# Expert jobs of 128 rows instead of 256 in a transformer kernel with two mixture-of-experts layers

## Chip, cores and metric

The kernel runs on one core of one Trainium2 chip. The metric is the device time of one execution in microseconds (us); the median of three runs is given. Everything is float32 unless a tile is said to be bfloat16.

## What is computed

The input x has 16 sequences of 256 rows with 128 features. Three layers of causal attention with 16 heads follow each other; the second and the third have an expert network behind them. The one that matters here is the second layer's: each row chooses its own two experts out of 8.

```
def _token_moe(h, gw, gb, w1, b1, w2, b2):
    cw = _combine_weights(h @ gw + gb)          # softmax over the two best of 8
    out = jnp.zeros_like(h)
    for e in range(E):
        out = out + _ffn(h, w1[e], b1[e], w2[e], b2[e]) * cw[..., e:e + 1]
    return out

def _ffn(h, w1, b1, w2, b2):                    # 128 -> 512 -> 128
    return jax.nn.gelu(h @ w1 + b1, approximate=False) @ w2 + b2

x = x + _layernorm(_attn_ref(_layernorm(x)))
x = x + _layernorm(_ffn_ref(_layernorm(x)))     # two layers: attention + experts
```

In the third layer a whole sequence chooses its two experts (`_seq_moe`). The change doesn't touch that one.

## The kernel before

The program has four parts on every engine. First come the first two attention layers (`run_steps` over `RUNS[0]`), one sequence after the other. In the second of them each row's normalised vector is sent to a buffer in HBM, `x_routed`, at a place that depends on its expert and on its rank among the rows of this expert; GpSimd (POOL) does that with indirect DMAs (`pool_send`). Then come the expert jobs of that layer, then the third attention layer, which begins by fetching each row's two results from `y_routed` (`pool_fetch`), then the experts of the third layer.

A job is a block of T = 256 consecutive rows of `x_routed` that belong to one expert. 4096 rows with two experts each are 8192 row visits; since every expert's last block may be partly empty, the program always runs JOBS = 2 x 16 + 8 = 40 jobs, the last of them on zeros if they aren't needed. `dve_tables` (L1014) works out on VectorE (DVE), in a chain in which each instruction waits for the one before, how many blocks each expert has, and from this the expert and first row of every job (`job_e`, `job_row`, L1043 to L1060). It also gives the place after each expert's last row (`pad_row`), where `pads` (L1293) writes a block of zeros, four experts from SyncE's queue (SP) and four from ScalarE's (ACT).

The jobs run as a software pipeline over five engines, each with its own loop made by `run_jobs` (L1199): two bodies written out, a loop of two bodies, and the last jobs written out.

- SP (`sp_jobs`, L1300): in the body of job j it reads job j+4's row from the table (`value_load`), waits until the transposes of job j+2 are done, and loads 256 rows into `xj[par]`, one of two buffers. Then it waits for job j's sum (`acc`) and stores `yj[par]` into `y_routed`.
- PE, the TensorE (`pe_jobs`, L1216): transposes the rows of job j+2 (`rows_T`, L1221, two instructions), makes the hidden layer of job j+1 (`pe_hidden`, L1150: four matmuls of 256 columns, each two instructions), and the output of job j (`pe_output`, L1161: eight matmuls of 128 columns, each two instructions). In the profile these stages are "W1" = L1150 and "W2" = L1161.
- ACT (`act_jobs`, L1241): copies job j+2's transposed rows out of PSUM with scale and bias (L1245), and does the four Gelu instructions of job j+1 (L1172).
- POOL (`pool_jobs`, L1262): reads job j+2's expert from the table, waits until job j's hidden layer is done, and copies the expert's w1 (512 elements in each partition) into `w1_job[par]` (L1180).
- DVE (`dve_jobs`, L1273): reads job j+2's expert (L1196), waits for job j's Gelu and copies b1 (L1193, 4 elements), waits for job j's output and adds b2 to it into `yj[par]` (L1280), waits for that add, and copies w2 (L1187, 512 elements) and b2 (L1188) of job j+2.

`need(engine, semaphore, value)` is a wait that is left out where the value is zero or less, `alone(engine)` a semaphore increment that is there to carry a wait. `times` gives the count at which a buffer's load or store is over. Each tile of two buffers has the index `par`, the parity of the job.

Of the kernel before, what the change touches and what calls it, by code (L numbers as in the profile page):

```python
# [15 lines left out]
P = 128  # L16
# [4 lines left out]
E = 8  # L21
# [22 lines left out]
def build(nc, x_in, w_qk, w_v, w_o, b_qk, b_v, b_o, ln1, ln2, gate_w, gate_b, e_w1, e_b1, e_w2, e_b2, out):  # L44
# [7 lines left out]
    MAXJ = B  # L52
    JOBS = TOP * B + E
    REG = (MAXJ + 1) * T
# [3 lines left out]
    with ExitStack() as ctx:  # L58
# [102 lines left out]
        tb = prob1[:, 0].rearrange("p h q -> p (h q)")  # L161
        assert max(JOBS * E, NT * TOP * E) <= HG * P
# [6 lines left out]
        zeros = sb("zeros", [P, 2, P])  # L169

        xj = oT[:, 0, 0:2].rearrange("p i (t d) -> p i t d", t=2)
# [5 lines left out]
        x_routed = nc.dram_tensor("x_routed", [E * REG + T, P], F32, kind="Internal").ap()  # L177
        y_routed = nc.dram_tensor("y_routed", [JOBS * T, P], F32, kind="Internal").ap()
# [24 lines left out]
        x_got = [sem("x_got0"), sem("x_got1")]  # L203
# [714 lines left out]
        def pool_fetch(i, n):  # L918

            u = i.v - 2 * B  # L920
            t, rank = divmod(n, TOP)
            if n == 0:
                pool.wait_ge(table, NTABLE)
                if isinstance(i.v, int) and i.b < 2:
                    for par in range(2):
                        pool.wait_ge(y_sent[par], 8 * JOBS)
# [87 lines left out]
        def dve_tables():  # L1014
# [19 lines left out]
            step(nc.vector.scalar_tensor_tensor(out=t, in0=t, scalar=1.0 / T,  # L1034
# [19 lines left out]
            step(nc.vector.scalar_tensor_tensor(out=row, in0=row, scalar=float(T), in1=spare, op0=ALU.mult,  # L1054
# [16 lines left out]
            step(nc.vector.scalar_tensor_tensor(out=flat[2], in0=flat[0], scalar=float(T), in1=flat[1],  # L1071
# [83 lines left out]
        def pe_output(j, par):  # L1155
# [10 lines left out]
        def act_gelu(j, par):  # L1166
            need(act, y_ps, j - 1)
            act.wait_ge(b1_got, j + 1)
            for c in range(FC):
                if c % 2 == 0:  # L1170
                    act.wait_ge(h_ps, 2 * j + c // 2 + 1)
                nc.scalar.activation(hid[:, par, c], bank[2 * par + c // 2][:, (c % 2) * T:(c % 2 + 1) * T],  # L1172
                                     ACT.Gelu, bias=b1_job[:, par, c:c + 1]).then_inc(gelu_done, 1)
# [38 lines left out]
        def times(j, par):  # L1212

            return 8 * (j + (2 if par == 0 else 1))

        def pe_jobs():  # L1216
            def rows_T(j, par):
                pe.wait_ge(x_got[par], times(j, par))
                need(pe, xjT_sb, j - 1)
                for t in range(2):  # L1220
                    m = nc.tensor.transpose(bank[6 + par][:, t * P:(t + 1) * P], xj[:, par, t], ident[:])  # L1221
                m.then_inc(xjT_ps, 1)

            def hidden(j, par):
                pe.wait_ge(xjT_sb, j + 1)
                pe_hidden(j, par, xjT[:, par])

            def body(j, par):
                if ahead(j, 2):
                    rows_T(j + 2, par)  # L1230
                if ahead(j, 1):
                    hidden(j + 1, 1 - par)
                pe_output(j, par)
# [7 lines left out]
        def act_jobs():  # L1241
            def rows_T(j, par):
                act.wait_ge(xjT_ps, j + 1)
                need(act, h_ps, 2 * j - 2)
                nc.scalar.activation(xjT[:, par], bank[6 + par][:, 0:T], ACT.Identity,  # L1245
                                     scale=ln2_s[:, 0, 0:1], bias=ln2_s[:, 0, 1:2]).then_inc(xjT_sb, 1)

            def body(j, par):
                if ahead(j, 2):
                    rows_T(j + 2, par)  # L1250
                if ahead(j, 1):
                    act_gelu(j + 1, 1 - par)
# [3 lines left out]
            act_gelu(0, 0)  # L1256
# [5 lines left out]
        def pool_jobs():  # L1262
            def body(j, par):
                if ahead(j, 2):
                    pool_w1(j + 2, par, entry(job_e, j + 2))
# [7 lines left out]
        def dve_jobs():  # L1273
            def body(j, par):
                if ahead(j, 2):
# [17 lines left out]
        def pads(eng, experts):  # L1293

            for e in experts:
                row = eng.value_load(pad_row[0:1, e:e + 1], min_val=0, max_val=E * REG - T)
                eng.dma_start(x_routed[bass.ds(row, T)].rearrange("(t p) d -> p t d", p=P), zeros[:])\
                   .then_inc(pad_dma, 16)

        def sp_jobs():  # L1300

            def load(j, par):
                row = nc.sync.value_load(entry(job_row, j), min_val=0, max_val=E * REG)
                need(sp, xjT_ps, j - 1)
                alone(sp)
                sp.dma_start(xj[:, par], x_routed[bass.ds(row, T)].rearrange("(t p) d -> p t d", p=P))\
                  .then_inc(x_got[par], 16)

            def body(j, par):
# [13 lines left out]
            for j in range(4):  # L1323
                load(j, j % 2)
            run_jobs(sp, body, 4)
# [139 lines left out]
        def _(_):  # L1465
            sp.dma_start(x_all[:, 0:8], x_dram[:, 0:8]).then_inc(x_first, 16)
            for t, d in ((ln1_s, ln1), (wqk_s, w_qk), (wv_s, w_v)):
# [3 lines left out]
            sp.dma_start(x_routed[E * REG:E * REG + T].rearrange("(t p) d -> p t d", p=P), zeros[:])\  # L1471
              .then_inc(zeros_dma, 16)
# [182 lines left out]
```

## Time and profile before

| | us |
|---|---|
| median of three runs | 1273.79 |
| lowest and highest of them | 1273.51, 1277.96 |
| the profiled execution's own time | 1271.35 |
| its span, from the first to the last instruction | 1269.6 |
| mean granted clock of TensorE in it | 0.943 of full speed |

The profile is of one execution. The busy time of an engine counts its data instructions; value loads, register operations, branches and semaphore waits are not in it, but they have rows of their own under the name of the queue (DVEq, SPq).
### The profile page before, as it was taken

How to read it: one execution, taken by the hardware profiler on the slowest of the kernel's cores; microseconds unless marked ns; L12 is line 12 of the kernel's file. 1: busy time of each engine (PE TensorE's matmuls, PEld its weight loads, DVE VectorE, ACT ScalarE, POOL GpSimd, SP SyncE). 2: the span in 40 equal slices, each digit the busy share in tenths (PEclk: the TensorE clock that was granted, in tenths of full speed). 3: DMA queues.
4: the chain of work that ended last, by engine and by line, in shares of the span. 5: the costliest groups of instructions: out<-in, count | busy, mean ns of one | idle time of the engine just before them, and what ended most of it. 6: DMA issues, size and time to landing. Idle time of an engine off the chain costs nothing. (4 is left out here: it accounts for less than half of the span.)

```text
span 1269.6 us, 36493 instructions
## 1 busy us (share of the span) xinstructions
PE 1064.3 (84%) x10172; PEld 795.5 (63%) x10267; DVE 936.9 (74%) x2774; ACT 767.8 (60%) x1745; POOL 663.6 (52%) x986
## 2 busy tenths in 40 slices
PE   1888999999999899998199997387888989959997
PEld 0565666666666666665199997255655656638996
DVE  3678999999988889997523332278889888865665
ACT  1566777777777777776066564156657667645554
POOL 3345565566556777776611111566676666422332
PEclk8899999999999999999599999589989899988999
DMA  5332111111112122211222222243221211100000
GB/s 148 93 96 78 51 49 38 42 49 52 53 52 59 45 64 63 67 51 37 75 63 70 70 70 71 56 115 103 76 65 39 65 47 55 53 2 9 17 21 21
DMA packets 120793, 74.57 MB, mean 59 GB/s; under 512 B 7936, under 2 KB 115712, under 8 KB 120704
## 3 DMA queue, kind: packets, MB, share of 16 engines
q1 hardware_dynamic: 101536, 54.48, 15.5%
q10 hardware_dynamic: 15072, 10.61, 2.9%
q0 software_dynamic: 4096, 8.40, 2.2%
q8 instruction: 43, 0.70, 0.2%
q14 instruction: 46, 0.38, 0.1%
HBM read 22.21 MB, written 12.71 MB: 28 GB/s over the span
## 5 line engine op out<-in xcount | busy, mean ns | idle before, releaser
L608 DVE TENSOR_REDUCE negm<-bank 128x2 f32<-128x512 f32 (+1 forms) x576 | 389.1, 679 | 84.2 <-PE bank L300 59.0
L496 ACT ACTIVATE prob<-bank 128x512 f32<-128x512 f32 x576 | 339.7, 595 | 126.6 <-PE bank L322 88.5
L889 POOL TENSOR_SCALAR_AFFINE_SELECT prob<-prob 128x512 f32<-128x512 f32 x384 | 248.3, 648 | 171.3 <-ACT prob L496 169.1
L341 PE MATMUL bank<-prob,vaug 128*32 128x256 f32 (+1 forms) x3072 | 168.7, 338 | 1.6 <-POOL prob L889 1.3
L308 PE MATMUL bank<-stack 126*128 126x256 bf16 x768 | 152.3, 280 | 0.0
L327 PE MATMUL bank<-stack 128*128 128x256 bf16 x768 | 150.7, 278 | 0.9 <-ACT prob L496 0.9
L1180 POOL COPY w_job<-w_s 128x512 f32 x72 | 47.1, 655 | 191.7 <-PE bank L1150 183.0
L1161 PEld LDWEIGHTS bank<-w_job,prob 128*128 128x128 f32 x1152 | 139.6, 192 | 3.6
L1161 PE MATMUL bank<-w_job,prob 128*128 128x128 f32 x1152 | 139.9, 275 | 0.0
L341 PEld LDWEIGHTS bank<-prob,vaug 128*32 128x32 f32 x3072 | 81.6, 111 | 78.5 <-issue 46.7
L1172 ACT ACTIVATE prob<-bank,b_job 128x256 f32<-128x256 f32 x288 | 118.2, 469 | 16.4 <-PE bank L1150 15.1
L304 PE MATMUL bank<-maskneg,identb 128*128 128x256 bf16 x384 | 109.2, 284 | 2.7 <-DVE negm L608 2.7
L507 ACT COPY mT<-bank 8x256 bf16<-8x256 bf16 x192 | 68.4, 356 | 55.7 <-PE bank L352 52.5
L322 PE MATMUL bank<-stack 128*128 128x128 bf16 x768 | 75.5, 220 | 21.3 <-DMA stack<-mT 19.1
L300 PE MATMUL bank<-stack 126*128 126x128 bf16 x768 | 75.9, 221 | 20.3 <-DMA stack<-parts 8.9
L327 PEld LDWEIGHTS bank<-stack 128*128 128x128 bf16 x768 | 75.3, 99 | 13.4 <-ACT prob L496 1.5
L352 PE MATMUL bank<-identb,mparts 128*8 128x128 bf16 x384 | 53.4, 221 | 35.8 <-DVE mparts L617 34.9
L914 POOL DMA_INDIRECT x_routed<-hk,x_at x64 | 64.9, 1014 | 34.5 <-DVE x_at L769 16.6
L308 PEld LDWEIGHTS bank<-stack 126*128 126x128 bf16 x768 | 77.3, 101 | 8.3 <-issue 0.6
L1150 PE MATMUL bank<-oT,w_job 128*128 128x256 f32 x320 | 77.4, 386 | 0.0
L300 PEld LDWEIGHTS bank<-stack 126*128 126x128 bf16 x768 | 60.5, 99 | 25.0 <-issue 1.7
L933 POOL DMA_INDIRECT y_got<-y_routed,y_at x64 | 63.7, 995 | 22.4 <-POOL y_at L930 12.3
(180 smaller groups left out, 2003.7 us busy)
## 6 DMA issues: line engine op xcount, KB each, us to landing
stack<-parts SPq DMA_DIRECT2D x288, 128.0 KB
w_s<-e_w ACTq DMA_DIRECT2D x32, 256.0 KB, 2.9
oT<-x_routed SPq DMA_DIRECT2D x40, 128.0 KB, 2.1
y_routed<-oT SPq DMA_DIRECT2D x40, 128.0 KB, 1.8
stack<-mT SPq DMA_DIRECT2D x192, 4.0 KB
out<-x_all SPq DMA_DIRECT2D x16, 128.0 KB, 1.8
b_all<-e_b ACTq DMA_DIRECT2D x2, 512.0 KB, 8.3
x_routed<-hk,x_at POOLq DMA_INDIRECT x64, 2.3
```

The source lines that it names most:

```text
L300: m = nc.tensor.matmul(o[:, h], q[:, p0 + h, 0:P], k[:, p0 + h, 0:P], start=False, stop=True, skip_group_check=True)
L304: nc.tensor.matmul(o[:, :, P:T], identb[:], maskneg[:, 0:2], start=True, stop=False, skip_group_check=True)
L308: m = nc.tensor.matmul(o[:, h], q[:, hh, P:T], k[:, hh, :], start=False, stop=True, skip_group_check=True)
L322: m = nc.tensor.matmul(bk[:, h * P:(h + 1) * P], k[:, p0 + h, P:T], q[:, p0 + h, P:T], start=True, stop=True)
L327: m = nc.tensor.matmul(bk[:, h * T:(h + 1) * T], k[:, hh, 0:P], q[:, hh, :], start=True, stop=True)
L341: m = nc.tensor.matmul(o, w, (prob0, prob1)[kb][:, g % 2, h], start=kb == 0, stop=kb == 1, skip_group_check=True)
L496: nc.scalar.activation(o, s, ACT.Exp, scale=SCALE).then_inc(exp_done, 1)
L608: nc.vector.tensor_reduce(o, s, AX.X, ALU.max, negate=True).then_inc(max_done, 1)
L889: nc.gpsimd.affine_select(out=t, in_=t, compare_op=ALU.is_ge, fill=0.0, base=0, pattern=[[0, HG], [1, P]], channel_multiplier=-1).then_inc ...
L1150: m = nc.tensor.matmul(bank[2 * par + c // 2][:, (c % 2) * T:(c % 2 + 1) * T], w1_job[:, par, c * P:(c + 1) * P], rows, start=True, stop=True)
L1161: m = nc.tensor.matmul(bank[4 + par][:, t * P:(t + 1) * P], hid[:, par, c, t * P:(t + 1) * P], w2_job[:, par, c], start=(c == 0), stop=(c ...
L1172: nc.scalar.activation(hid[:, par, c], bank[2 * par + c // 2][:, (c % 2) * T:(c % 2 + 1) * T], ACT.Gelu, bias=b1_job[:, par, c:c + 1]).the ...
```

## The change

The jobs have P = 128 rows. There are JOBS = 2 x 32 + 8 = 72 of them, and MAXJ, the most blocks that one expert can have, is 32. A job has one transpose, four hidden matmuls of 128 columns and four output matmuls, and its instructions on ACT and DVE (L1245, L1172, L1280) work on 128 columns. The copies of w1, w2, b1 and b2 per job are as large as before. `x_got` has four semaphores and `xj` four buffers of 128 rows; rows are loaded six jobs ahead, after the transposes of the job two ahead. Results of two jobs lie side by side in `yj`, and SP stores them together, in the second one's body. Loops have four bodies, with four jobs written out before and eight behind. The tables are 72 entries long, and the pads are blocks of 128 rows.

```diff
-    MAXJ = B
-    JOBS = TOP * B + E
-    REG = (MAXJ + 1) * T
+    MAXJ = NT
+    JOBS = TOP * NT + E
+    REG = (MAXJ + 1) * P
...
-        x_got = [sem("x_got0"), sem("x_got1")]
+        x_got = [sem("x_got0"), sem("x_got1"), sem("x_got2"), sem("x_got3")]
...
-        def pe_hidden(j, par, rows):
+        def pe_hidden(j, par, rows, width=T):
...
-                m = nc.tensor.matmul(bank[2 * par + c // 2][:, (c % 2) * T:(c % 2 + 1) * T],
+                m = nc.tensor.matmul(bank[2 * par + c // 2][:, (c % 2) * T:(c % 2) * T + width],
                                      w1_job[:, par, c * P:(c + 1) * P], rows, start=True, stop=True)
...
-            for t in range(2):
+            for t in range(tiles_of):
...
-        def run_jobs(eng, body, ahead=2):
-
-            for j in range(2):
+        def run_jobs(eng, body):
+
+            for j in range(4):
                 body(j, j)
-            with eng.Fori(2, JOBS - ahead - 1, 2) as j:
-                for par in range(2):
-                    body(j + par, par)
-            for j in range(JOBS - ahead, JOBS):
-                body(j, j % 2)
+            with eng.Fori(4, JOBS - 11, 4) as j:
+                for m in range(4):
+                    body(j + m, m)
+            for j in range(JOBS - 8, JOBS):
+                body(j, j % 4)
...
-            def rows_T(j, par):
-                pe.wait_ge(x_got[par], times(j, par))
+            def rows_T(j, m):
+                par = m % 2
+                pe.wait_ge(x_got[m], times(j, m))
                 need(pe, xjT_sb, j - 1)
-                for t in range(2):
-                    m = nc.tensor.transpose(bank[6 + par][:, t * P:(t + 1) * P], xj[:, par, t], ident[:])
-                m.then_inc(xjT_ps, 1)
+                nc.tensor.transpose(bank[6 + par][:, 0:P], xj[:, m], ident[:]).then_inc(xjT_ps, 1)
...
                 dve.wait_ge(y_ps, j + 1)
-                need(dve, y_sent[par], times(j, par) - 16)
-                nc.vector.tensor_tensor(yj[:, par], bank[4 + par][:, 0:T].rearrange("p (t d) -> p t d", t=2),
-                                        b2_job[:, par:par + 1].to_broadcast([P, 2, P]),
+                need(dve, y_sent[m // 2], times(j, m) - 16)
+                nc.vector.tensor_tensor(yj[:, m // 2, par], bank[4 + par][:, 0:P], b2_job[:, par],
                                         ALU.add).then_inc(acc, 2)
...
-            def load(j, par):
+            def load(j, m):
                 row = nc.sync.value_load(entry(job_row, j), min_val=0, max_val=E * REG)
-                need(sp, xjT_ps, j - 1)
+                need(sp, xjT_ps, j - 3)
                 alone(sp)
-                sp.dma_start(xj[:, par], x_routed[bass.ds(row, T)].rearrange("(t p) d -> p t d", p=P))\
-                  .then_inc(x_got[par], 16)
-
-            def body(j, par):
-                if ahead(j, 4):
-                    load(j + 4, par)
-                sp.wait_ge(acc, 2 * j + 2)
-                alone(sp)
-                at = bass.ds(j * T, T)
-                sp.dma_start(y_routed[at].rearrange("(t p) d -> p t d", p=P), yj[:, par]).then_inc(y_sent[par], 16)
+                sp.dma_start(xj[:, m], x_routed[bass.ds(row, P)]).then_inc(x_got[m], 16)
+
+            def body(j, m):
+                if ahead(j, 6):
+                    load(j + 6, (m + 2) % 4)
+                if m % 2:
+                    sp.wait_ge(acc, 2 * j + 2)
+                    alone(sp)
+                    at = bass.ds((j - 1) * P, T)
+                    sp.dma_start(y_routed[at].rearrange("(t p) d -> p t d", p=P), yj[:, m // 2])\
+                      .then_inc(y_sent[m // 2], 16)
```

The third layer's experts call `pe_hidden`, `pe_output` and `act_gelu` with the old widths.

## Rows read from the trace of the kernel before

**Rows 1.** The page's head: span, and PE's busy time, share and instructions.
```profile
span 1269.6 us, 36493 instructions
PE 1064.3 (84%) x10172; PEld 795.5 (63%) x10267; DVE 936.9 (74%) x2774; ACT 767.8 (60%) x1745; POOL 663.6 (52%) x986
```

**Rows 2.** View by stretches: us, busy of PE, PEld, DVE, ACT, POOL, clock, DMA.
```profile
640.60:783.00 142.40, 142.40 (x994) 134.51 (x993) 51.36 (x152) 85.55 (x193) 22.69 (x37) 1.00 0.24 68
```

**Rows 3.** Timeline of PE, one job: start us, us, engine, line, operation, tiles.
```profile
691.18 0.38 PE L1221 MATMUL bank<-ident,oT 128*128 128x128 f32 x2
691.40 1.89 PE L1150 MATMUL bank<-oT,w_job 128*128 128x256 f32 x8
693.13 1.95 PE L1161 MATMUL bank<-w_job,prob 128*128 128x128 f32 x16
694.91 0.38 PE L1221 MATMUL bank<-ident,oT 128*128 128x128 f32 x2
```

**Rows 4.** Waits from 640 to 780 us: us in total, times, longest.
```profile
POOL w_job L1180 <- PE bank L1150: 113.6, 37, 3.4
DVE oT L1280 <- PE bank L1161: 53.5, 37, 2.2
```

**Rows 5.** Timeline of the table, the pads and the first transposes.
```profile
619.68 0.49 DVE L1047 TENSOR_TENSOR prob<-iota_j,js 128x320 f32<-128x320 f32 x1
...
624.57 4.11 SPq L1297 DMA_DIRECT2D x_routed<-zeros  x4
...
633.79 0.66 PE L1221 MATMUL bank<-ident,oT 128*128 128x128 f32 x2 [19.08 <-DMA oT<-x_routed]
```

**Rows 6.** Timeline: the last matmuls of the jobs.
```profile
782.47 3.73 PE L1161 MATMUL bank<-w_job,prob 128*128 128x128 f32 x32
```

**Rows 7.** Groups of instructions by shape, whole program: busy us, mean ns, idle before.
```profile
L1172 ACT ACTIVATE prob<-bank,b_job 128x256 f32<-128x256 f32 x288 | 118.2, 469 | 16.4 <-PE bank L1150 15.1
L502 ACT COPY oT<-bank 128x256 f32<-128x256 f32 x192 | 70.9, 369 | 5.3 <-PE bank L341 4.8
...
L538 ACT COPY hn<-bank 128x128 f32<-128x128 f32 x3 | 0.6, 274 | 0.4 <-PE bank L532 0.4
...
L627 DVE TENSOR_TENSOR on<-bank,rden 128x128 f32<-128x128 f32 x96 | 28.0, 291 | 3.3
```

**Rows 8.** The page's DMA issues: KB each, median us from issue to landing.
```profile
oT<-x_routed SPq DMA_DIRECT2D x40, 128.0 KB, 2.1
```

**Rows 9.** Value loads of DVE (L1196) and SP (L1303): ns, least, median, most.
```profile
L1196 DVEq TENSOR_LOAD <-job_e x37: 300/304/317, 643.7 to 778.3; - x37
...
L1303 SPq TENSOR_LOAD <-job_row x35: 263/271/556, 644.3 to 771.1; - x35
```

**Rows 10.** Timeline of all engines over two jobs.
```profile
691.44 0.42 DVE L1280 TENSOR_TENSOR oT<-bank,oT 128x256 f32<-128x256 f32 x1 [1.69 <-PE bank L1161]
...
692.11 0.43 DVE L1187 COPY w_job<-w_s 128x512 f32 x1 [0.24 <-DVE oT L1280]
692.46 0.22 DVE L1188 COPY oT<-b_all 128x128 f32 x1
692.47 1.70 ACT L1172 ACTIVATE prob<-bank,b_job 128x256 f32<-128x256 f32 x4 [0.21 <-PE bank L1150]
...
693.54 0.61 POOL L1180 COPY w_job<-w_s 128x512 f32 x1 [3.03 <-PE bank L1150]
693.57 0.61 DVE L1193 COPY b_job<-b_s 128x4 f32 x1 [0.89 <-ACT prob L1172]
694.03 0.39 SPq L1306 DMA_DIRECT2D oT<-x_routed  x1
...
695.96 0.43 DVE L1187 COPY w_job<-w_s 128x512 f32 x1 [0.25 <-DVE oT L1280]
...
697.05 0.17 DVE L1193 COPY b_job<-b_s 128x4 f32 x1 [0.53 <-ACT prob L1172]
697.36 0.61 POOL L1180 COPY w_job<-w_s 128x512 f32 x1 [3.21 <-PE bank L1150]
```

More of the change, by code:

```diff
@@ L160, in build @@
         earlier = sb("earlier", [P, E, E])
-        tb = prob1[:, 0].rearrange("p h q -> p (h q)")
-        assert max(JOBS * E, NT * TOP * E) <= HG * P
+        tb = prob1[:].rearrange("p g h q -> p (g h q)")
+        assert max(JOBS * E, NT * TOP * E) <= 2 * HG * P and JOBS % 4 == 0
         nj, js = sb("nj", [P, E]), sb("js", [P, E])
@@ L1033, in dve_tables @@
             step(nc.vector.tensor_copy(t, counts[:].unsqueeze(2).to_broadcast([P, E, MAXJ])))
-            step(nc.vector.scalar_tensor_tensor(out=t, in0=t, scalar=1.0 / T,
+            step(nc.vector.scalar_tensor_tensor(out=t, in0=t, scalar=1.0 / P,
                                                 in1=iota_j[:, 0:MAXJ].unsqueeze(1).to_broadcast([P, E, MAXJ]),
@@ L1053, in dve_tables @@
             step(nc.vector.tensor_scalar(spare, mask, 1.0, float(REG), ALU.subtract, ALU.mult))
-            step(nc.vector.scalar_tensor_tensor(out=row, in0=row, scalar=float(T), in1=spare, op0=ALU.mult,
+            step(nc.vector.scalar_tensor_tensor(out=row, in0=row, scalar=float(P), in1=spare, op0=ALU.mult,
                                                 op1=ALU.add))
@@ L1070, in dve_tables @@
             step(nc.vector.tensor_reduce(flat[0], t, AX.X, ALU.add))
-            step(nc.vector.scalar_tensor_tensor(out=flat[2], in0=flat[0], scalar=float(T), in1=flat[1],
+            step(nc.vector.scalar_tensor_tensor(out=flat[2], in0=flat[0], scalar=float(P), in1=flat[1],
                                                 op0=ALU.mult, op1=ALU.add))
@@ L1244, in rows_T, with body @@
                 need(act, h_ps, 2 * j - 2)
-                nc.scalar.activation(xjT[:, par], bank[6 + par][:, 0:T], ACT.Identity,
+                nc.scalar.activation(xjT[:, par, 0:P], bank[6 + par][:, 0:P], ACT.Identity,
                                      scale=ln2_s[:, 0, 0:1], bias=ln2_s[:, 0, 1:2]).then_inc(xjT_sb, 1)
-            def body(j, par):
+            def body(j, m):
+                par = m % 2
                 if ahead(j, 2):
@@ L1251, in body @@
                 if ahead(j, 1):
-                    act_gelu(j + 1, 1 - par)
+                    act_gelu(j + 1, 1 - par, P)
             rows_T(0, 0)
             rows_T(1, 1)
-            act_gelu(0, 0)
+            act_gelu(0, 0, P)
             run_jobs(act, body)
@@ L1262, in pool_jobs, with body @@
         def pool_jobs():
-            def body(j, par):
+            def body(j, m):
                 if ahead(j, 2):
-                    pool_w1(j + 2, par, entry(job_e, j + 2))
+                    pool_w1(j + 2, m % 2, entry(job_e, j + 2))
             pool.wait_ge(expert_ld[0], 32 * E)
@@ L1273, in dve_jobs, with body @@
         def dve_jobs():
-            def body(j, par):
+            def body(j, m):
+                par = m % 2
                 if ahead(j, 2):
@@ L1295, in pads, with body @@
             for e in experts:
-                row = eng.value_load(pad_row[0:1, e:e + 1], min_val=0, max_val=E * REG - T)
-                eng.dma_start(x_routed[bass.ds(row, T)].rearrange("(t p) d -> p t d", p=P), zeros[:])\
+                row = eng.value_load(pad_row[0:1, e:e + 1], min_val=0, max_val=E * REG - P)
+                eng.dma_start(x_routed[bass.ds(row, P)], zeros[:])\
                    .then_inc(pad_dma, 16)
         def sp_jobs():
-            def load(j, par):
+            def load(j, m):
                 row = nc.sync.value_load(entry(job_row, j), min_val=0, max_val=E * REG)
-                need(sp, xjT_ps, j - 1)
+                need(sp, xjT_ps, j - 3)
                 alone(sp)
-                sp.dma_start(xj[:, par], x_routed[bass.ds(row, T)].rearrange("(t p) d -> p t d", p=P))\
-                  .then_inc(x_got[par], 16)
-            def body(j, par):
-                if ahead(j, 4):
-                    load(j + 4, par)
-                sp.wait_ge(acc, 2 * j + 2)
-                alone(sp)
-                at = bass.ds(j * T, T)
-                sp.dma_start(y_routed[at].rearrange("(t p) d -> p t d", p=P), yj[:, par]).then_inc(y_sent[par], 16)
+                sp.dma_start(xj[:, m], x_routed[bass.ds(row, P)]).then_inc(x_got[m], 16)
+            def body(j, m):
+                if ahead(j, 6):
[6 more added lines that the diff above has]
+                      .then_inc(y_sent[m // 2], 16)
             sp.wait_ge(table, NTABLE_JOBS)
@@ L1322, in sp_jobs @@
                 sp.wait_ge(x_sent[par], 8 * 2 * TOP * B)
-            for j in range(4):
-                load(j, j % 2)
-            run_jobs(sp, body, 4)
+            for j in range(6):
+                load(j, j % 4)
+            run_jobs(sp, body)
         def pe_experts():
```

31 lines of the change are left out of this document (16 added, 15 removed).

## The prediction

> **What bounds the kernel now.** I first asked where in the program the change acts. Only the stretch of the expert jobs, and the table that plans it, are touched. The busy shares of the whole program [rows 1] therefore say little; the view by stretches says more. Between 640.6 and 783.0 us TensorE is busy without a gap at a granted clock of 1.00 (its upper level, 2.4 GHz), while DVE works for 51 of 142 us and POOL for 23 [rows 2]. The timeline of one job shows its period: the two transposes start at 691.18, the W1 matmuls at 691.40, the W2 matmuls at 693.13, the next job's transposes at 694.91, so 0.22 + 1.73 + 1.78 = 3.73 us for 256 rows [rows 3]. The waits say the same from the other side: POOL waits 3.1 us a job for W1's end and DVE 1.4 us for W2's end [rows 4]. PE sets the pace, and every other engine has slack. The question is how much of it is left when a job is half as long.
>
> **What a job costs PE afterwards.** W2's sixteen matmul instructions have 128 columns and start every 1.78/16 = 0.111 us; W1's eight have 256 and start every 0.216 us [rows 3]. So an instruction costs in proportion to its columns, and 128-column W1 instructions take the pitch of W2's. A new job is one transpose (0.11), eight W1 (0.89) and eight W2 instructions (0.89), 1.89 us. 72 jobs are 136.1 us against 40 x 3.73 = 149.2: PE has 9216 rows to do, not 10240. From the first transpose at 633.79 to the end of the last matmuls (782.47 + 3.73 = 786.2) the stage lasts 152.4 us, 3.2 more than 40 periods: for the first jobs, when the engines behind PE fill up [rows 5, 6]. I take 3.5 for the new stage (3 to 5: the same latencies with less PE work beside them). If PE sets the pace, the stage lasts 139.6 us, 12.8 less.
>
> **What comes before it.** The table instructions over jobs x experts grow from 320 to 576 elements. One of 320 takes 0.49 us [rows 5], one of 128 takes 0.29 (L627, another form of tensor_tensor) [rows 7], so about 1 ns an element: four of them add 1.0 us, the first three (256 elements for 128) 0.4, seven over 72 instead of 40 elements 0.2. These all lie on the path, since pads and job rows wait for them. The pads are half as large but their issue (four in 4.11 us on SP [rows 5]) stays; I give them 0.1. Sum +1.5 us (1.2 to 1.7). Loads are 64 KB instead of 128 and asked for with a lead of four jobs instead of two, 7.6 us as against 7.5, where 128 KB landed in 2.1 [rows 8]: PE's work hides them. The last store holds the same 256 rows, so the way from the last matmul to the first fetch of y stays; a shorter last add, 0.13, is left out.
>
> **The other engines at 1.89 us a job.** ACT: a Gelu of 256 columns takes 0.47 [rows 7], four of them 1.70 from start to end [rows 10], so they start every 0.41. A copy of 256 columns takes 0.37 and one of 128 takes 0.27 [rows 7], so 0.1 goes from each: 4 x 0.31, and at most 0.47 for the fifth instruction (L1245), are 1.7 us. It fits, without much air. POOL: a copy of 0.61 and a value load, no longer than 1.2. SP: in two jobs two loads (value load 0.27 to 0.56 [rows 9], registers and a wait, an issue of 0.39 [rows 10], together 1.2 to 1.5 each) and now one store (0.7), 3.1 to 3.7 against 3.78: it just fits, because the stores were halved. Its new store waits for the second job's add, and two loads are queued behind it; they are asked for four jobs before PE wants them, so nothing waits for that.
>
> DVE is the tight one, for its work is per job and not per row. Its chain in a loop body is strictly in order: add, own wait, copy of w2, copy of b2, value load of the expert, copy of b1, next add. From add to w2 copy it took 0.67 (691.44 to 692.11), 0.54 with a 128-column add (0.29 [rows 7] for 0.42). From w2 copy to b1 copy it took 1.09 where no branch lies between (695.96 to 697.05) and 1.46 where the loop ends (692.11 to 693.57) [rows 10]. b1 itself takes 0.17. So a body free of waits lasts 0.54 + 1.09 + 0.17 = 1.80, and the one with the loop's end 2.17. Four bodies to a loop give a mean of 1.89; if the three others carry the register work that today only the first body has (0.1), 1.97. DVE's own pace is 1.89 to 1.97, PE's is 1.89. What PE would wait for first is w2. It and b2 are ready 0.57 after the start of the w2 copy (692.11 to 692.46 and 0.22) [rows 10], so 0.2 + 0.54 + 0.57 = 1.3 us after the end of the output before it in the same buffer. W2 of that next job starts 1.89 + 1.0 = 2.9 us after the same end. With a wake-up of 0.1 to 0.2, DVE may fall 1.4 us behind before PE notices.
>
> **What makes it worse: two copies that exclude each other.** At 693.54 POOL starts its copy of w1 and holds until 694.15; DVE's 4-element copy of b1, started at 693.57, takes 0.61 and ends at 694.18. The same copy one job later, with POOL idle, takes 0.17 [rows 10]. So DVE stands still while POOL copies. Today this costs nothing; at 1.89 us a job it does. POOL starts 0.41 to 0.50 after W2's first matmul [rows 3, 10]. Counted from the end of W2, DVE adds at 0.2, copies w2 from 0.74, and would copy b1 at 1.83; POOL holds from 1.4 to 2.1. b1 then ends at 2.1, the next add starts 0.2 to 0.3 late, which is harmless. The loop's end adds 0.28 every fourth job, and only if the other three bodies are under 1.89 is it given back. By the mean of the two bounds (1.93) DVE slips 0.15 a loop. When it is 0.9 behind, its w2 copy begins inside POOL's window, it loses the rest of 1.4 at one blow, and PE waits for w2. In that state: w2 ready at 0, W2's matmuls at 0.2, the hidden matmuls of two jobs later end 1.89 later, POOL copies from 2.5 to 3.15; b1 of the next body ends with it, and the w2 after that is ready 0.54 + 0.57 later, 4.3 in all with the gaps. Two jobs in 4.3 us is 2.16 us a job, whatever DVE could do alone, and it feeds itself as long as one body in two is over 2.0.
>
> "SBUF — State Buffer" of the Trainium skill, section "SBUF: two separate sides", says that VectorE in a 2-port mode and GpSimd share one port pair as an exclusive lock, held for the whole instruction. Taken alone, that is the rule that speaks against this change, for it puts 72 pairs of such copies where 40 were. By this, the trace agrees (0.61 for 0.17).
>
> **The forecast.** From a lag of 0.35 to 0.9 at 0.15 a loop is four loops; with the first four jobs the lock begins at about job 20, and some 50 jobs take 2.16 - 1.89 = 0.27 more: +13.3. Sum: -12.8 + 1.5 + 13.3 = +2.0 us. Against the profiled execution's own time, 1271.35 us (span 1269.6 [rows 1]), that is 1273.4; the median of the runs lies 2.4 above that execution, so I say 1276. A difference of 0.5% (6.4 us) is about what a measurement of this kernel can tell from none. In general the change is 72 p - 147.4 us for a mean period p: zero at 2.05, slower by over 0.5% from 2.14, faster by over 0.5% below 1.96.
>
> **The rivals.**
>
> (a) PE keeps the pace. For it: DVE's lower bound is exactly 1.89, the lag before PE notices is large, and DVE is in the lock only after a slip. Then 72 x 1.89 gives -11.3 us, 1262.5. Against it: the loop's end, and collisions that are certain in each job.
>
> (b) DVE's chain is longer than two jobs in 4.3 us, from the first jobs on. The place is its value load, 0.30 now [rows 9]; SP's load of the same table takes 0.27 or 0.56, by what runs beside it. With 0.25 more on it, and a collision of w2 or b1 in each body, a body takes 2.3: 72 x 2.3 - 147.4 = +18, 1292. It decides from a mean of 2.14, which the lock of 2.16 from the first jobs on would also just reach (+8, 1282).
>
> (c) SP is the bound: two loads at 1.5 and a store with its loop branch make 3.9 to 4.0 for two jobs, 1.97 us a job, -5.5 us, 1268. It would show no lock, and it is inside the band of no change.
>
> (d) The change doesn't shorten PE's job because 128-column W1 instructions don't pair with their weight loads. Speaking against it: W2's do, at the same shapes [rows 3]. I give it next to nothing.
>
> **How the numbers follow.** The forecast, with the lock setting in late or broken at times and (c) beside it, 0.37, own range 1268 to 1280; (a) 0.36; (b) and the lock from the start 0.27. So faster 0.36, same 0.37, slower 0.27. The range reaches down to (a)'s figure with the gain of a shorter fill, 1261, and up to a mean period of 2.26, 1289; beyond it lies the worse half of (b).
>
> **What would show it.** PE's first transpose 1.5 us later than 633.8. W1 instructions at 0.11 pitch. A busy share of PE of 87 to 95% in the stage, with waits for w2's copy (L1187 or L1188) that begin around job 20; PE at 100% would be (a). b1 copies of more than 0.4 us in at least every second job, ending with POOL's copy. SP's waits for x rows absent. It would be wrong if the DVE bodies outside the loop's end took under 1.8 or over 2.1 us, if POOL's and DVE's copies turned out to fall apart of themselves, or if PE waited for x_got.

## The result, and the profile after

| | before | after |
|---|---|---|
| median of the runs, us | 1273.88 | 1261.20 |
| lowest and highest | 1273.51, 1277.96 | 1259.02, 1262.36 |
| span of the profiled execution | 1269.6 | 1258.4 |

The changed kernel is faster by 12.7 us. The ratio to before is 0.9891, with a 95% interval of 0.9866 to 0.9917. The forecast was 1276, 2 us slower than before; what happened is nearly rival (a), 1262.5, PE keeps the pace.

The first view is the same as [rows 2], over the changed kernel's jobs (us, busy us and instructions of PE, PEld, DVE, ACT, POOL, then granted clock, DMA share and GB/s):

```profile
640.40:771.00 130.60, 130.60 (x1170) 130.59 (x1168) 82.97 (x276) 105.23 (x344) 43.68 (x68) 1.00 0.23 67
```

PE is still busy throughout, and at a granted clock of 1.00. DVE went from 36% of the stretch to 64%, ACT from 60% to 81%. The timeline of PE shows the new job beside [rows 3], early in the stage and late in it:

```profile
664.03 0.27 PE L1222 MATMUL bank<-ident,oT 128*128 128x128 f32 x1
664.14 1.06 PE L1150 MATMUL bank<-oT,w_job 128*128 128x128 f32 x8
665.03 1.06 PE L1161 MATMUL bank<-w_job,prob 128*128 128x128 f32 x8
665.93 0.27 PE L1222 MATMUL bank<-ident,oT 128*128 128x128 f32 x1
...
732.56 1.06 PE L1150 MATMUL bank<-oT,w_job 128*128 128x128 f32 x8
733.46 1.13 PE L1161 MATMUL bank<-w_job,prob 128*128 128x128 f32 x8
734.42 0.27 PE L1222 MATMUL bank<-ident,oT 128*128 128x128 f32 x1
```

A job is 0.11 + 0.89 + 0.90 = 1.90 us. Late in the stage one job in four has a gap: its W2 instructions take 1.13 us and not 1.06, and the next transpose comes 0.07 us later. The waits over the jobs answer to [rows 4] (us in total, times, longest):

```profile
POOL w_job L1181 <- PE bank L1150: 86.1, 68, 1.6
...
ACT prob L1172 <- DVE b_job L1194: 11.4, 27, 0.8
...
DVE oT L1283 <- PE bank L1161: 0.3, 1, 0.3
```

DVE, which waited for W2 in every job before (53.5 us), has one such wait left in this view. Its slack is used up. The start and the end of the stage answer to [rows 5, 6]:

```profile
619.22 0.76 DVE L1047 TENSOR_TENSOR prob<-iota_j,js 128x576 f32<-128x576 f32 x1
...
625.48 3.67 SPq L1299 DMA_DIRECT2D x_routed<-zeros  x4
...
633.12 0.45 PE L1222 MATMUL bank<-ident,oT 128*128 128x128 f32 x1 [19.20 <-DMA oT<-x_routed]
...
771.56 2.21 PE L1161 MATMUL bank<-w_job,prob 128*128 128x128 f32 x16
...
776.75 0.19 POOL L930 COPY y_at<-y_at_all 128x4 uint32<-128x4 uint32 x1 [7.85 <-DMA y_routed<-oT]
```

From first transpose to last matmul the stage took 633.12 to 773.77, 140.65 us, where it took 152.4. The spans differ by 11.2 us: -11.75 from this stage, -0.8 from the stages ahead of it, +0.1 from the table and the pads, +0.3 from the wait for the last store and +0.9 from all that follows.

### The profile page after: what moved, and what is told of

Its sections match the earlier page's. It is cut to its first block and busy times, and to the rows that moved or that the text cites. A ratio compares the mean times of both kernels' runs of the same rounds, so it can differ in the third digit from the quotient of the medians.

```text
span 1258.4 us, 38248 instructions
## 1 busy us (share of the span) xinstructions
PE 1048.2 (83%) x10356; PEld 791.0 (63%) x10451; DVE 974.2 (77%) x2902; ACT 789.2 (63%) x1905; POOL 683.7 (54%) x1018
## 5 line engine op out<-in xcount | busy, mean ns | idle before, releaser
L1181 POOL COPY w_job<-w_s 128x512 f32 x104 | 67.7, 651 | 164.6 <-PE bank L1150 156.0
L1172 ACT ACTIVATE prob<-bank,b_job 128x128 f32<-128x128 f32 (+1 forms) x416 | 133.4, 398 | 24.7 <-PE bank L1150 11.8
L1161 PE MATMUL bank<-w_job,prob 128*128 128x128 f32 x1088 | 138.9, 276 | 0.1
L1161 PEld LDWEIGHTS bank<-w_job,prob 128*128 128x128 f32 x1088 | 132.2, 192 | 2.1 <-issue 0.5
L1150 PE MATMUL bank<-oT,w_job 128*128 128x128 f32 x576 | 77.6, 279 | 0.0
```

What stands on the lines that cost most here:

```text
L1161: m = nc.tensor.matmul(bank[4 + par][:, t * P:(t + 1) * P], hid[:, par, c, t * P:(t + 1) * P], w2_job[:, par, c], start=(c == 0), stop=(c ...
L1172: nc.scalar.activation(hid[:, par, c, 0:width], bank[2 * par + c // 2][:, (c % 2) * T:(c % 2) * T + width], ACT.Gelu, bias=b1_job[:, par, ...
```

## The experiments

All kernels were timed beside the kernel before on the same chip. Its own runs spread from 1268 to 1278 us in these sessions, so differences of a few us between variants are read from the trace, not from the medians: from the stage (first transpose to last matmul, 152.4 us before, 140.65 in the changed kernel) and from the distance of the adds in it. The stage itself is good to about 1 us: three kernels with the changed kernel's pace took 140.65, 140.45 and 141.4.

**Where the gain comes from.** Two kernels take the size of a job and the number of rows apart. The first has jobs of 256 rows, but only 36 of them:

```diff
-    JOBS = TOP * B + E
+    JOBS = TOP * B + E - 4
```

> The kernel before with 36 jobs of 256 rows instead of 40: the four jobs left out are zero rows for these inputs (35 are needed), so nothing of the result is missing. Theory R (PE sets the pace in both kernels, and the whole gain is the 1024 rows that it no longer works on): four periods of 3.73 us less, 1273.9 - 14.9 = 1259.0, as fast as the changed kernel or a little faster. Theory S (short jobs gain by themselves, through shorter filling, smaller pads and paired stores, and fewer rows is the smaller part): at least half of the change's 12.7 us stays out, 1265 or more.

Measured: 1260.97 us, ratio 0.9897 (0.9867 to 0.9927). The second has jobs of 128 rows, but as many rows as before:

```diff
-    JOBS = TOP * NT + E
+    JOBS = TOP * NT + E + 8
```

> The changed kernel with 80 jobs of 128 rows instead of 72, so that it works on 10240 rows as the kernel before does; the eight added jobs are zero rows. Theory R: eight periods of 1.90 to 1.92 us more, 1261.2 + 15.2 = 1276.4, that is 0 to 4 us slower than the kernel before. Theory S: it stays clearly faster than the kernel before, 1270 or less.

Measured: 1278.89 us, ratio 1.0036 (1.0018 to 1.0053), slightly slower than before. So theory R holds: with 9216 rows both job sizes take 1261 us, with 10240 rows they take 1274 and 1279. Short jobs gain nothing by themselves; in the stage they even cost 3.3 us, with few rows (137.3 in the first kernel, 140.65 in the changed one) as with many (152.4 before, 155.7 in the second). They waste fewer rows in each expert's last block, and that is the gain. (36 jobs of 256 rows are enough for these inputs only.)

**The same jobs on the old structure.** Two x buffers with loads four jobs ahead, a store for each job, loops of two bodies:

```diff
-            with eng.Fori(4, JOBS - 11, 4) as j:
-                for m in range(4):
-                    body(j + m, m)
+            with eng.Fori(2, JOBS - ahead - 1, 2) as j:
+                for par in range(2):
+                    body(j + par, par)
...
-                if ahead(j, 6):
-                    load(j + 6, (m + 2) % 4)
-                if m % 2:
-                    sp.wait_ge(acc, 2 * j + 2)
+                if ahead(j, 4):
+                    load(j + 4, m)
+                sp.wait_ge(acc, 2 * j + 2)
...
```

> Jobs of 128 rows with everything else as before: two x buffers loaded four jobs ahead, a store for every job, loops of two bodies. In the changed kernel's trace the DVE bodies of a loop take 2.29, 1.75, 1.75 and 1.87 us. Theory D (DVE's chain of value load, waits and copies is as long as PE's job, so a loop's end every second job and not every fourth makes it the bound): (2.29 + 1.80) / 2 = 2.05 us a job, 72 x (2.05 - 1.90) = +11, 1272. Theory Q (SP is the bound, with two loads and two stores for two jobs, 3.9 to 4.5 us): up to 2.25 a job, 1261.2 + 25 = 1286. Theory N (the other parts of the change do nothing, PE keeps the pace): 1261.

Measured: 1281.43 us, ratio 1.0058 (1.0036 to 1.0081), 20 us slower than the changed kernel and slower than before. The queue of SP in this kernel, DMA issues only (start us, us):

```profile
709.57 0.34 SPq L1308 DMA_DIRECT2D oT<-x_routed  x1
710.26 0.35 SPq L1315 DMA_DIRECT2D y_routed<-oT  x1
711.91 0.34 SPq L1308 DMA_DIRECT2D oT<-x_routed  x1
712.67 0.35 SPq L1315 DMA_DIRECT2D y_routed<-oT  x1
713.95 0.34 SPq L1308 DMA_DIRECT2D oT<-x_routed  x1
```

Two loads and two stores take 4.38 us here, 2.17 a job in the mean of the stage, and SP's queue waited for nobody but 4 times from 640 to 790 us, for 3.9 us. It is SP, theory Q, and not DVE.

**One store for each job** (buffers, lead and loop as in the changed kernel):

```diff
-                if m % 2:
-                    sp.wait_ge(acc, 2 * j + 2)
-                    alone(sp)
-                    at = bass.ds((j - 1) * P, T)
-                    sp.dma_start(y_routed[at].rearrange("(t p) d -> p t d", p=P), yj[:, m // 2])\
-                      .then_inc(y_sent[m // 2], 16)
+                sp.wait_ge(acc, 2 * j + 2)
+                alone(sp)
+                sp.dma_start(y_routed[bass.ds(j * P, P)], yj[:, m // 2, m % 2]).then_inc(y_sent[m], 16)
```

> The changed kernel with a store of 64 KB for every job instead of one of 128 KB for two; loads, buffers and loop are those of the changed kernel. In the run of 128-row jobs on the old structure SP's queue took 1.28 us from a store's issue to the next load's (1.65 over a loop's end) and 0.70 from a load's to a store's. Theory Q (SP's queue is the bound as soon as each job has a load and a store): four jobs take 4 x (1.28 + 0.70) + 0.37 = 8.3 us, 2.07 a job, 72 x (2.07 - 1.90) = +12, 1273. Theory L (what slowed that run was the short lead of the loads, not the number of SP's instructions): 1261.

Measured: 1271.04 us, ratio 0.9989 (0.9966 to 1.0012); four loads stand 8.42 us apart (740.96 to 749.38), and from 700 us on SP's queue has no wait at all. The paired store is worth 8 us of stage (148.6 against 140.65), 10 by the medians, of a gain of 12.7.

**Two x buffers, four jobs ahead** (paired store and loop of four as in the changed kernel):

```diff
-                need(sp, xjT_ps, j - 3)
+                need(sp, xjT_ps, j - 1)
...
-                sp.dma_start(xj[:, m], x_routed[bass.ds(row, P)]).then_inc(x_got[m], 16)
+                sp.dma_start(xj[:, m % 2], x_routed[bass.ds(row, P)]).then_inc(x_got[m % 2], 16)
...
-                if ahead(j, 6):
-                    load(j + 6, (m + 2) % 4)
+                if ahead(j, 4):
+                    load(j + 4, m)
```

> The changed kernel with two x buffers, loaded four jobs ahead as before the change, instead of four buffers and six jobs ahead; store for two jobs and loop of four as in the changed kernel. Theory L (the lead is needed: the first load of a pair is queued behind the store, 0.3 us after the add, then 0.65 for the store, 1.2 for the value load and registers and 1.9 to land, 4.1 to 4.3 us after W2's end, and PE wants it after two jobs, 3.8): 2.1 us a job, 1261.2 + 15 = 1276, with PE waiting for x rows every second job. Theory K (four jobs of lead are enough, the extra buffers do nothing): 1261.

Measured: 1277.68 us, ratio 1.0038 (1.0022 to 1.0055), 2.11 us a job in the trace. The waits of this kernel from 640 to 775 us have two lines that the changed kernel's have not (the two overlap, weight load and matmul):

```profile
PEld bank L1222 <- DMA oT<-x_routed: 9.7, 13, 0.9
...
PE bank L1222 <- DMA oT<-x_routed: 8.5, 14, 1.3
```

Theory L holds in its time and in who waits. In one point it doesn't: PE stands still before one transpose in four and not in two, 0.7 to 0.8 us each time, some 11 of the 14 us that the stage lost. The longer lead is worth those 14 us, more than the paired store, and each is needed with the other in place.

**Eight bodies to a loop:**

```diff
-            with eng.Fori(4, JOBS - 11, 4) as j:
-                for m in range(4):
-                    body(j + m, m)
-            for j in range(JOBS - 8, JOBS):
+            turns = (JOBS - 12) // 8
+            with eng.Fori(4, 8 * turns - 3, 8) as j:
+                for m in range(8):
+                    body(j + m, m % 4)
+            for j in range(4 + 8 * turns, JOBS):
```

> The changed kernel with eight bodies to a loop instead of four. Theory D: DVE's mean body falls from 1.915 to (2.29 + 7 x 1.79) / 8 = 1.85, below PE's 1.895, and PE never waits: 1 to 1.5 us less, about 1260. Theory N (DVE isn't the bound anywhere): 1261.2 within 0.3. Either way the stretch of 640 to 770 us shows mean job periods: 1.895 throughout by D, unchanged by N.

Measured: 1262.95 us, ratio 0.9914 (0.9888 to 0.994): not distinguishable from the changed kernel by time. In the traces the adds of the jobs stand 1.895 us apart instead of 1.906, and the stage is 0.7 us shorter. The stage alone couldn't show so little, the distance of the adds does: 0.011 us a job is 0.8 us over the stage. DVE's pace costs something in the changed kernel, but about 1 us at most.

**Collisions of POOL and DVE taken away.** POOL copies 4 elements of w1 instead of 512:

```diff
-            nc.gpsimd.tensor_copy(w1_job[:, par:par + 1], w1_s[:, bass.ds(e, 1)]).then_inc(w1_got, 1)
+            nc.gpsimd.tensor_copy(w1_job[:, par:par + 1, 0:width], w1_s[:, bass.ds(e, 1), 0:width])\
+              .then_inc(w1_got, 1)
```

> The changed kernel with POOL's copy of w1 cut to 4 of its 512 elements in all jobs but the first two, so most of the copies that exclude DVE's are gone. What this leaves out: the jobs compute with w1 of the first two jobs. Theory D (in the changed kernel the collisions fall on DVE's copy of w2, whose stretch of 0.1 to 0.4 us is hidden behind DVE's own value load, so they cost nothing): time unchanged, 1261 within 1, DVE's adds still 7.66 us apart for four jobs in the second half, all w2 copies at 0.43. Theory C (the collisions of the prediction cost DVE time, only less than forecast): DVE's four bodies get shorter than 7.58 and PE never waits, 1259 to 1260.

Measured: 1263.55 us, ratio 0.9922 (0.9893 to 0.9951). The adds have the same mean distance as in the changed kernel, 1.906 us, and four of them take 7.66 us late in the stage in both, while w2's copies take 0.43 to 0.46 instead of 0.55 in the mean (0.88 at most). Theory D: in the changed kernel the collisions cost nothing.

**DVE's queue lengthened**, by one or two semaphore increments a job:

```diff
                 if ahead(j, 2):
                     e = expert_of(entry(job_e, j + 2))
                     dve_b1(0, j + 2, par, e)
+                for _ in range(1):
+                    alone(dve)
                 dve.wait_ge(y_ps, j + 1)
```

> The changed kernel with one more semaphore increment in DVE's queue before each job's add, about 0.1 us of queue time a job (the trace will show how much). Theory D (DVE's mean body, 1.915 us, is already at PE's 1.895): nearly all of it appears, 72 x 0.1 = +6 to +7, 1267 to 1268. Theory M (the lock of the prediction sets in when bodies are over 2.0): 2.16 us a job from an early job on, +15 to +18, 1277. Theory N (DVE has slack): 1261.

Measured: 1272.88 us, ratio 0.9988 (0.9972 to 1.0004). One instruction of 0.1 us in DVE's queue takes back almost the whole gain by the medians; in the trace the stage took 148.6 us, 7.9 more than the changed kernel's. The other 4 us lie outside the stage, and no run explains them. Four jobs take 8.27 us. The timeline of this kernel shows more than the increment:

```profile
707.23 0.61 POOL L1181 COPY w_job<-w_s 128x512 f32 x1 [1.28 <-PE bank L1150]
707.26 0.61 DVE L1194 COPY b_job<-b_s 128x4 f32 x1 [0.90 <-ACT prob L1172]
707.78 0.28 DVE L1285 TENSOR_TENSOR oT<-bank,oT 128x128 f32<-128x128 f32 x1
...
709.13 0.61 POOL L1181 COPY w_job<-w_s 128x512 f32 x1 [1.28 <-PE bank L1150]
709.38 0.38 DVE L1194 COPY b_job<-b_s 128x4 f32 x1 [0.52 <-ACT prob L1172]
709.68 0.28 DVE L1285 TENSOR_TENSOR oT<-bank,oT 128x128 f32<-128x128 f32 x1
```

POOL's copy has moved onto b1's, as in the collision of [rows 10], and the add stands right behind b1. To tell the two costs apart, the same kernel with POOL's copies cut to 4 elements:

> The run with one more semaphore increment in DVE's queue, and POOL's copy of w1 cut to 4 of 512 elements as well (the jobs compute with w1 of the first two jobs; that is what is left out). With the increment alone four adds took 8.27 us, 2.07 a job, although the queue time of the four bodies adds up to 8.01, and b1 copies of 0.61 and 0.38 us stood in two of the four bodies. Theory C2 (once a body passes 2.0 us, POOL's copy catches DVE's copy of b1, and that is not hidden because the add waits behind it): without the copies 2.00 a job, 72 x 0.07 = 5 us less than 1272.9, 1268. Theory D2 (the queue time is all, the collisions are hidden here too): 2.07 a job, 1273.

Measured: 1269.74 us, ratio 0.9965 (0.9943 to 0.9987), 3.1 us less by the medians; four jobs take 8.02 us and no b1 copy is longer than 0.18. The stage took 146.5 us: of the 7.9 us that one increment costs there, some 6 are the queue's own time and some 2 are collisions (0.06 a job, once the pattern of four bodies is steady). The four bodies show which collisions count. With whole copies they take 1.90, 1.83, 1.96 and 2.59 us, without them 1.85, 1.84, 1.96 and 2.38: the two with a stretched b1 copy (0.38 and 0.61 us) are longer, and the one whose only stretched copy is w2's (0.57 us) is not.

> The changed kernel with two more semaphore increments in DVE's queue before each add. Bodies free of waits are then 2.10 us on average. Theory M (the lock of the prediction, two jobs in 4.3 us whatever DVE could do alone): 2.16 a job with b1 copies over 0.3 in every second body, 72 x (2.16 - 1.90) = +19, 1280. Theory D2 (queue time alone): 2.10, +14, 1275.5. If collisions add to the queue time rather than set a floor: 2.10 + 0.07 = 2.17, also 1280; the run with POOL's copies cut and the b1 durations tell these apart from D2, not from each other.

Measured: 1274.13 us, ratio 1.0015 (0.9992 to 1.0038), 8.41 us for four jobs, 2.10 each.

> Two more semaphore increments in DVE's queue, and POOL's copy of w1 cut to 4 elements (w1 of the first two jobs is used throughout). By all theories of DVE's queue 2.10 us a job, 1275.5; b1 copies all at 0.17. The difference to the run with whole copies is what the collisions cost at this pace.

Measured: 1275.48 us, ratio 1.0018 (0.9999 to 1.0037), and 2.10 us a job too. With two increments the collisions cost nothing again once the pattern is steady, although two b1 copies in four are still stretched in the kernel with whole copies (its stage took 153.1 us, this one's 152.4; the difference lies in the first jobs). Its timeline shows why:

```profile
706.59 0.61 POOL L1181 COPY w_job<-w_s 128x512 f32 x1 [1.37 <-PE bank L1150]
...
706.88 0.35 DVE L1194 COPY b_job<-b_s 128x4 f32 x1 [0.97 <-ACT prob L1172]
...
707.29 0.29 DVE L1285 TENSOR_TENSOR oT<-bank,oT 128x128 f32<-128x128 f32 x1
```

The copy is over at 707.23, and the queue needs until 707.29 anyway for the two increments and the wait ahead of the add. Theory M, the floor of 4.3 us for two jobs, has fallen: it would have given 2.16 in the former. A collision costs what the stretched copy exceeds the queue's own work behind it, so it depends on which copy POOL meets and how much of it, and doesn't rise with the length of a body.

**A version meant to be better.** 71 jobs are always enough, and eight bodies to a loop keep DVE off the path:

```diff
-    JOBS = TOP * NT + E
+    JOBS = TOP * NT + E - 1
...
                       .then_inc(y_sent[m // 2], 16)
+                elif isinstance(j, int) and j == JOBS - 1:
+                    sp.wait_ge(acc, 2 * j + 2)
+                    alone(sp)
+                    sp.dma_start(y_routed[bass.ds(j * P, P)], yj[:, m // 2, 0]).then_inc(y_sent[m // 2], 16)
```

> A version meant to beat the changed kernel: 71 jobs, for 8192 row visits in 8 experts fill at most 64 + 7 blocks of 128 rows, and eight bodies to a loop, which keeps DVE's mean body under PE's. The last job is stored alone. Theory R: one period of 1.90 and the 0.7 us of stage that the loop of eight saved less: 2.6 us below the changed kernel, 1258.6. If neither matters, 1261.2. The runs of one kernel spread over 3 to 7 us, so the median may not show it; the stage in the trace should: 140.6 - 2.6 = 138.0 us from first transpose to last add.

Measured: 1263.38 us, ratio 0.9923 (0.9895 to 0.9952). The stage took 138.9 us, but the end of it looks like this:

```profile
772.58 0.41 ACTq L1562 DMA_DIRECT2D b_all<-e_b  x1
...
774.72 0.34 SPq L1323 DMA_DIRECT2D y_routed<-oT  x1
779.50 0.19 POOL L930 COPY y_at<-y_at_all 128x4 uint32<-128x4 uint32 x1 [10.12 <-DMA y_routed<-oT]
```

The last store, though only 64 KB, was waited for until 4.8 us after its issue. (This profile is of a run of 1267.9 us, 4.5 above the median.) The suspect is the 512 KB load of b2, issued 2.1 us ahead of it. Two more kernels issue it after the last store has landed, the first as the only edit to the changed kernel, the second on top of 71 jobs and loops of eight:

```diff
             act.wait_ge(w2_got, JOBS)
+            for par in range(2):
+                act.wait_ge(y_sent[par], 4 * JOBS)
```

> The changed kernel, with the 512 KB load of the third layer's b2 on ACT's queue issued only after the last job's store has landed (it is issued 2.1 us ahead of that store now, at 772.10 against 774.2). Theory B (this load holds up the last store: from the last add to POOL's first step of the next part took 3.0 us in the changed kernel, 2.7 before, and 3.7, 4.1 and 5.3 in the variants): 2.7 us or less there in the profile, and 0.3 to 1 us off the time, 1260.5. Theory N: 3.0, no change.

> 71 jobs, eight bodies to a loop, and the b2 load after the last store. Without the last edit the stage took 138.9 us, 1.7 less than the changed kernel's, but the wait for the last store took 5.3 instead of 3.0 and ate that. Theory B: 2.7 us or less there, so 2.0 us below the changed kernel in stage and wait together, 1259. Theory N (the long wait has another cause): above 4 us there, 1262 to 1263.

Measured: 1263.96 us (ratio 0.9926, 0.9911 to 0.9941) and 1261.90 us (0.9909, 0.9893 to 0.9926). From the end of the last W2 matmul to POOL's first step (this is the stretch that the expectations call "from the last add") it took 2.55 us in the first and 3.05 in the second, against 3.00 in the changed kernel and 5.26 without the edit. That is in favour of theory B, from one profile each, though 3.05 misses its 2.7, and it stays open why the stretch is 0.3 us longer than before in one kernel with this load ahead of the store and 2.6 in another. The second kernel's stage took 138.1 us. The time didn't follow: in both profiles the part from POOL's first step on took 3 to 4 us more than in the changed kernel's (485.4 and 484.7 against 481.7). Over all variants, whose code there is the same, it lies between 479.8 and 486.7. Why that part varies was not settled. No version tried here is clearly faster than the changed kernel.

## Why the prediction was wrong, step by step

**What held.** PE's job of 1.89 us (measured 1.90), its 72 x 1.89 = 136 us plus 3.5 for filling (139.6 forecast for PE's pace, 140.65 measured). DVE as the tight engine: its four bodies were put at 7.56 to 7.88 us and took 7.66 to PE's 7.58. Singly they were less well met: 1.75 twice and 1.87 for the forecast 1.80 to 1.90, 2.29 at the loop's end for 2.17; so the prediction's own sign of being wrong, bodies under 1.8, did appear. The lag of DVE did grow, to 0.8 us at job 12 and 1.3 at job 40, and from there on PE waits 0.07 us in every fourth job. SP was put at 3.1 to 3.7 of 3.8 us for two jobs: its queue waited 5.0 of the 115 us from 650 to 765, which leaves 3.6, and the need for the halved stores came out in the run with single stores. Rival (b) says that SP's value load takes 0.27 or 0.56 "by what runs beside it"; in both traces the long ones are exactly those right behind the loop's branch.

**The step that failed** is in the paragraph on the copies that exclude each other: "its w2 copy begins inside POOL's window, it loses the rest of 1.4 at one blow". The copy does begin in that window, and is stretched as foreseen. This is DVE and POOL in the changed kernel at the 13th and 14th job:

```profile
663.12 0.29 DVE L1283 TENSOR_TENSOR oT<-bank,oT 128x128 f32<-128x128 f32 x1
...
663.55 0.61 POOL L1181 COPY w_job<-w_s 128x512 f32 x1 [1.28 <-PE bank L1150]
663.65 0.79 DVE L1188 COPY w_job<-w_s 128x512 f32 x1 [0.24 <-DVE oT L1283]
...
664.36 0.21 DVE L1189 COPY oT<-b_all 128x128 f32 x1
...
664.73 0.17 DVE L1194 COPY b_job<-b_s 128x4 f32 x1 [0.16 <-issue]
664.87 0.29 DVE L1283 TENSOR_TENSOR oT<-bank,oT 128x128 f32<-128x128 f32 x1
```

w2's copy takes 0.79 us instead of 0.43, b2's follows later, and b1's still starts at 664.73, 1.08 us after w2's start, as in [rows 10] (1.09). The 1.09 us between the two copies are not the copies' own time. They are the queue's: the value load of 0.30, the register instructions and the wait, which run while the data copy is stretched. A stretch of 0.36 us fits beneath them. The forecast added the stretch to the chain, and from that came the jump to PE's limit, the lock and its 13.3 us, of which nothing was measured. The run with POOL's copies cut shows it: same pace without any collision.

**What PE waits for** was wrong too. The prediction says "What PE would wait for first is w2", from a lag of 1.4 us on. At the largest lag, 1.3, the changed kernel's 43rd job shows something else:

```profile
716.50 0.17 DVE L1194 COPY b_job<-b_s 128x4 f32 x1 [0.72 <-issue]
...
716.84 1.14 ACT L1172 ACTIVATE prob<-bank,b_job 128x128 f32<-128x128 f32 x4 [0.75 <-DVE b_job L1194]
...
717.26 0.43 DVE L1188 COPY w_job<-w_s 128x512 f32 x1 [0.24 <-DVE oT L1283]
717.60 0.22 DVE L1189 COPY oT<-b_all 128x128 f32 x1
...
718.14 1.13 PE L1161 MATMUL bank<-w_job,prob 128*128 128x128 f32 x8
```

w2 and b2 of this job were ready at 717.82. The Gelus, which had waited for b1, ended at 717.98, and W2's first weight load came at 718.11, 0.08 later than the pitch of those before it. PE is reached through b1 and ACT, not through w2. With one increment more in DVE's queue the waits (650 to 775 us) say so by name, and no line has PE waiting for w2:

```profile
PE bank L1161 <- ACT prob L1172: 5.1, 12, 0.4
```

With two it is still the Gelus (5.2 us, 14 times); only with two increments and POOL's copies cut are w2 and b2 (L1189) named in their place (4.3 us, 13 times).

**The lock itself** was wrong as a floor; that a collision on b1 can delay the next add was right. It was worked out for a body over 2.0 us. The changed kernel's bodies are 1.915 in the mean, and b1's copy starts ahead of POOL's. One increment more, and bodies of 2.00 became 2.07, with b1 copies of 0.61 and 0.38. At 2.10 nothing was added. The forecast took a collision on b1 in every second job, paid in full; in the runs POOL meets another copy from body to body, and part or all of the stretch is hidden.

**Smaller terms.** The table grew by 1.7 us as forecast (1.5), but the first transpose came 0.1 later and not 1.5: from the last table entry to the first transpose it took 1.6 us less, which the half-sized pads (four issues in 3.67 instead of 4.11 us) may explain in part. Pads had been given 0.1. It is no chance of one profile: from the end of the instruction that writes `job_row` (L1059) to the first transpose it took 8.9 to 9.6 us in all kernels with 128-row blocks, and 10.5 and 12.0 in the two with 256. Why was not tested. DVE's pace costs 0.7 us of stage, by the loop of eight. The wait for the last store, forecast as unchanged, is 0.3 longer.

**The chances.** The bound for a gain, a mean period under 1.96, was right, and DVE's bounds of 1.89 to 1.97 lay almost wholly on that side; only the lock, for which no row showed that a stretched copy delays the chain, moved the forecast across. The range went down to 1261 and 1261.2 was measured, just inside; its low end had no room for the variation between runs, so that it held is luck.

## What to carry to other kernels

Cutting a job in half halves only what is per row; count, for every queue, the instructions that are per job (value loads, register steps, semaphore waits, DMA issues), and give the queue that carries both loads and stores half as many of the latter. Before a collision is added to a chain, look whether the next instruction waits for the stretched one or only for the queue: the gap in the timeline that is no data instruction is where a stretch hides. When an engine falls behind, ask of each thing that it makes when the others need it: the one with the least room here was b1 for the Gelus, a copy of 4 elements. A kernel whose second engine is within 1% of the first can lose its gain to a single queue instruction, so measure that slack by adding one.

## What the runs showed of the hardware

- One semaphore increment in DVE's queue takes 0.1 us of the chain (four bodies of 8.02 instead of 7.66 us). With the pace at the limit, collisions included, it cost 7.9 us of stage over 72 jobs, 0.15 a job once the pattern was steady, and 11.7 us by the medians.
- DVE's queue goes on with its value load and register instructions while its data copy is held up by POOL's: b1's copy starts 1.08 us after w2's, whether w2's takes 0.79 us (663.65 to 664.73) or 0.43 (0.43 and 1.08 with POOL's copies cut).
- POOL's and DVE's copies exclude each other in both directions of order, also for copies of 512 elements: behind POOL's, DVE's took 0.79 us instead of 0.43, and behind DVE's, POOL's took 0.86 instead of 0.61. DVE's add with one operand in PSUM kept its 0.29 us under a copy of POOL (changed kernel's timeline):

```profile
665.41 0.43 DVE L1188 COPY w_job<-w_s 128x512 f32 x1 [0.24 <-DVE oT L1283]
665.45 0.86 POOL L1181 COPY w_job<-w_s 128x512 f32 x1 [1.28 <-PE bank L1150]
...
731.97 0.61 POOL L1181 COPY w_job<-w_s 128x512 f32 x1 [1.28 <-PE bank L1150]
732.04 0.29 DVE L1283 TENSOR_TENSOR oT<-bank,oT 128x128 f32<-128x128 f32 x1
```

  That agrees with the section "SBUF: two separate sides" of "SBUF — State Buffer" in the Trainium skill, by which engines contend only for the port pair that VectorE and GpSimd share, and never for VectorE's own.
- 128-column instructions keep their price: 0.111 us each for W1 and W2, where the 256-column ones took 0.216.
